# Routing MoE plus masked pooling on one core: where VectorE waits for the last operation of a table piece

## The chip, the cores and the metric

The kernel runs on one core of a Trainium2 chip. The metric is device time in microseconds (us); three runs of the kernel before gave 456.40, 456.65 and 457.12, so the median is 456.65. PE is TensorE, DVE is VectorE, ACT is ScalarE, POOL is GpSimd, SP is SyncE. "DVEq" in a row is DVE's own sequencer: register, load and wait instructions that it carries out itself and doesn't hand to the vector datapath.

## The reference, cut to what matters

The input is x, 8 batches of 512 tokens of 256 features. Layer 0: `u = zX * lap_x(x) + zY * lap_y(x) + zR * x * (1 - x)`, then a mixture of 8 experts with the best two chosen for each token:

```
logits = u @ router_weight; top_vals, top_idx = top_k(logits, 2); scores = softmax(top_vals)
gu = u @ gate_up_proj[e] + gate_up_proj_bias[e]            # 256 -> 512, gate and up interleaved
act = (clip(up, -7, 7) + 1) * min(gate, 7) * sigmoid(1.702 * min(gate, 7))
x = x + sum over the two experts of score * (act @ down_proj[e] + down_proj_bias[e])
```

Layer 1: scores `tanh(x @ W1 + b1) @ v`, a softmax over them under one of three masks (prefix, postfix, all but itself; one kind per batch), the pooled rows divided by the count of allowed positions, and an fp8-rounded product with `kernel`, whose result is added to x.

## The kernel before, in words

Stage A (0 to about 106 us) computes u, the router and each token's slots, and scatters the rows of u into per-expert regions of device memory. Stage B, the expert loop (about 106 to 317 us), takes NB = 71 blocks of 128 rows, two blocks to a step (`steps`; PAIRED is 68, the last three blocks stand alone). Stage C (from about 321 us) adds the weighted expert rows to X, computes the scores, the masked pooling and the fp8 product.

All engines run programs written out in full, one after the other, with semaphores between them. `instruction.then_inc(sem, 1)` raises a semaphore when the instruction is done; `dve.wait_ge(sem, n)` stands ahead of the next DVE instruction in program order, whatever that is.

What DVE does in iteration g of the expert loop (L1428 to L1444), in this order: `biased(g-1, 1)` (adds the bias to the second block of the last pair, L1337), `act_low(g-2)` (the low half of the transposed activation, L1360), `clipped(g-1)` (L1345, L1346), `rows_low(g+1)` (the low half of the transposed rows, L1325, and two small L1329), `activated(g-1)` (L1354), `biased(g, 0)` (L1337 for the first block), and then, for each block n of step g-1, `late_blocks(n)` and `tables_beside(n)`. These two do nothing for most n. For some even n they do one small piece of work that doesn't belong to the experts' own chain:

- `late_blocks`: n = 2, 4, 6, 8, 10, 12, 14: the experts and rows of the last 39 blocks, and the two weights of each token.
- `tables_beside`: n = 20 to 34 and 40 to 48 in twos: the kinds, scales, the rounded fp8 weights, the counts and the row and column tables of stage C.

Below, "piece n" is the work for block n. Pieces are short: one to four operations on DVE. Within a piece each operation that needs the one before it goes through `then` (semaphore `route_step`, L1211) or `table` (semaphore `table_step`, L1365). Both raise the semaphore by the instruction and write a wait for it behind the instruction at once. So in 17 of the pieces the last thing is a wait for the piece's own last operation.

Behind the piece DVE comes to `biased(g, 1)`, which begins with reading the number of the block's expert from on-chip memory into a register:

```
expert = dve.value_load(block_expert[0:1, n:n + 1], min_val=0, max_val=E - 1)   # L1335
dve.wait_ge(gu_psum, n + 1)                                                      # L1336
dve.tensor_tensor(gu_sum[...], gu_banks[...], gu_bias[:, ds(expert), :]..., ALU.add)   # L1337
```

[...]

PE's order in iteration g (L958 to L972): `gate_up(g, 0)`, `rows_transposed(g+1)`, `down(g-2)`, which needs `act_low(g-2)` of DVE (the wait shows at L949), `gate_up(g, 1)`, `act_transposed(g-1)`, which needs `activated(g-1)` of DVE (L940). ACT's order: `transposed_act(g-2)` (L680), `activate(g-1)` (L675), `rows_rounded(g+1)` (L670), `finish_down(g-2)` (L688). POOL scatters each finished block (L594), SP fetches the rows of blocks up to eight ahead (L486). When all blocks have been stored, SP loads `picks` (L524) and stage C begins.

PE waits for `table_step` once (L1002), up to the two steps of piece 20. Nobody but DVE waits for `route_step`.

Of the kernel before, what the change touches and what calls it, by code (L numbers as in the profile page):

```python
# [25 lines left out]
ALU = mybir.AluOpType  # L26
# [5 lines left out]
I32 = mybir.dt.int32  # L32
U32 = mybir.dt.uint32

P = 128
ALPHA, LIMIT = 1.702, 7.0
NEG = -1.0e30
EXPONENT_BITS = 0x7F800000
FP8_LEAST_NORMAL = 2.0 ** -6
FP8_GRID = 1.5 * 2.0 ** 20  # L40
# [39 lines left out]
def adaln_ffn_kernel(nc, x, zx, zy, zr, kinds, router_w, gate_up_w, gate_up_b, down_w, down_b,  # L80
                     w1, b1, v, ffn_k, in_scale, k_scale, ffn_b, out):
    B, S, H = x.shape
    E = router_w.shape[1]
# [23 lines left out]
    CAP = T + P  # L107
    CUT = B - 3
    FIRST_NB = (2 * CUT * S - E * (P - 1)) // P
    LATE_NB = NB - FIRST_NB  # L110
# [15 lines left out]
    with ExitStack() as ctx:  # L126
# [13 lines left out]
        tok_w = sb("tok_w", [P, 2, NT])  # L140
        ident = sb("ident", [P, P])

        with ExitStack() as ab:
# [13 lines left out]
            ends = sb("ends", [P, 10, E])  # L157
            ends_i = sb("ends_i", [P, 2, E], I32)
            base_f = sb("base_f", [P, E])
            odds = sb("odds", [P, 3, NT])  # L160
            blk_f = sb("blk_f", [P, NB])
# [39 lines left out]
            with ExitStack() as b_:  # L201
# [12 lines left out]
                kind_row = sb("kind_row", [1, 4, B])  # L214
# [3 lines left out]
                kind_col = sb("kind_col", [P, 8])  # L218
                spread = sb("spread", [P, QS, R], F32R)
                masks = sb("masks", [P, 3, P], BF16)  # L220
                zeros = sb("zeros", [P, P], BF16)
                counts = sb("counts", [P, 3, TB])
# [906 lines left out]
        def _(dve):  # L1129
# [78 lines left out]

            done = [0]

            def then(instruction):  # L1211
                done[0] += 1
                instruction.then_inc(route_step, 1)
                dve.wait_ge(route_step, done[0])

            def best_two(n):
# [68 lines left out]

            def late_blocks(n):
                late = blk_past[:, 0:LATE_NB]
                if n == 2:
                    dve.tensor_tensor(pads_at[:], ends[0:1, COUNT], base_f[0:1], ALU.add).then_inc(addresses_ready, 1)
                    rounded_down(P - 1, FULL)  # L1290
                if n == 4:
                    then(dve.tensor_tensor(ends_of(PADDED), ends_of(FULL), ends_of(TAKEN), ALU.subtract))
                    dve.memset(ends[:, JUMP, E - 1:E], float(E * CAP))
                    then(dve.tensor_tensor(ends[:, JUMP, 0:E - 1], ends[:, TAKEN, 1:E], ends[:, FULL, 0:E - 1],
                                           ALU.subtract))
                    then(dve.tensor_scalar(ends[:, JUMP, 0:E - 1], ends[:, JUMP, 0:E - 1], float(CAP), None, ALU.add))
                if n == 6:
                    then(dve.tensor_tensor_scan(ends_of(END), ends_of(ONE), ends_of(PADDED), 0.0, ALU.mult, ALU.add))
                    then(dve.tensor_tensor(late, blk_f[:, 0:LATE_NB].unsqueeze(2).broadcast_to([P, LATE_NB, E]),
                                           ends_of(END).unsqueeze(1).broadcast_to([P, LATE_NB, E]), ALU.is_ge))  # L1300
                if n == 8:
                    then(dve.tensor_reduce(blk_at[:, 0:LATE_NB], late, AX.X, ALU.add))
                    then(dve.tensor_scalar(block_is[:, FIRST_NB:NB], blk_at[:, 0:LATE_NB], float(E - 1), None, ALU.min))
                    dve.tensor_copy(block_expert[:, FIRST_NB:NB], block_is[0:1, FIRST_NB:NB]).then_inc(experts_ready, 1)
                if n == 10:
                    then(dve.tensor_tensor(late, late, ends_of(JUMP).unsqueeze(1).broadcast_to([P, LATE_NB, E]), ALU.mult))
                if n == 12:
                    then(dve.tensor_reduce(blk_at[:, 0:LATE_NB], late, AX.X, ALU.add))
                    then(dve.tensor_tensor(blk_at[:, 0:LATE_NB], blk_at[:, 0:LATE_NB], blk_f[:, 0:LATE_NB], ALU.add))
                    dve.tensor_scalar(block_row[:, FIRST_NB:NB], blk_at[0:1, 0:LATE_NB], ends[0:1, TAKEN, 0:1],  # L1310
                                      float(E * CAP), ALU.add, ALU.min).then_inc(addresses_ready, 1)
                if n == 14:
                    dve.wait_ge(odds_ready, 1)
                    then(dve.tensor_scalar(odds[:, 2], odds[:, 1], 1.0, None, ALU.add))
                    then(dve.reciprocal(tok_w[:, 0, :], odds[:, 2]))
                    then(dve.tensor_tensor(tok_w[:, 1, :], odds[:, 1], tok_w[:, 0, :], ALU.mult))

            x_low(0)
            straight(B, 2, step_a)
# [42 lines left out]

            tdone = [0]

            def table(instruction):  # L1365
                tdone[0] += 1
                instruction.then_inc(table_step, 1)
                dve.wait_ge(table_step, tdone[0])

            COLUMN, COLUMN_BATCH, ELSE, BELOW, ABOVE, OWN = range(6)  # L1370
            ROW, ROW_BATCH, KIND, PREFIX, POSTFIX, CLOZE, ONLY_POST, ONLY_PRE = range(8)

            def tables_beside(n):
                if n == 20:
                    dve.wait_ge(c_loaded, 16 * C_DMAS)
                    dve.memset(one[:], 1.0)
                    table(dve.tensor_copy(kind_row[:, 0, :], kind_row_i[:, 0, :]))
                    table(dve.tensor_copy(kind_rep[:], kind_row[:, 0, :].unsqueeze(1).unsqueeze(3).broadcast_to([1, QS, B, TB])))
                    assert tdone[0] == KIND_STEPS
                if n == 22:  # L1380
                    dve.tensor_scalar(kind_row[:, 1, :], kind_row[:, 0, :], 0.0, -2.0, ALU.is_equal, ALU.mult)
                    table(dve.tensor_scalar(kind_row[:, 2, :], kind_row[:, 0, :], 1.0, None, ALU.is_equal))
                    table(dve.tensor_tensor(kind_row[:, 1, :], kind_row[:, 1, :], kind_row[:, 2, :], ALU.subtract))
                if n == 24:
                    table(dve.tensor_scalar(kind_row_i[:, 1, :], kind_row[:, 1, :], 2.0, None, ALU.add))
                    table(dve.reciprocal(scales[:, 3:5], scales[:, 0:2]))
                    table(dve.tensor_tensor(scales[:, 2:3], scales[:, 0:1], scales[:, 1:2], ALU.mult))
                if n == 26:
                    table(dve.tensor_scalar(k_scaled[:], k_raw[:], scales[:, 4:5], None, ALU.mult))
                if n == 28:  # L1390
                    table(dve.tensor_scalar(k_grid[:].bitcast(I32), k_scaled[:].bitcast(I32), EXPONENT_BITS, None,
                                            ALU.bitwise_and))
                if n == 30:
                    table(dve.tensor_scalar(k_grid[:], k_grid[:], FP8_LEAST_NORMAL, FP8_GRID, ALU.max, ALU.mult))
                if n == 32:
                    table(dve.tensor_tensor(k_scaled[:], k_scaled[:], k_grid[:], ALU.add))
                if n == 34:
                    table(dve.tensor_tensor(k_quant[:], k_scaled[:], k_grid[:], ALU.subtract))
                if n == 40:
                    dve.wait_ge(tables, POOL_TABLES)  # L1400
                    table(dve.tensor_copy(counts[:, 0, :], counts_i[:]))
                    dve.tensor_scalar(counts[:, 1, :], counts[:, 0, :], -1.0, float(S + 1), ALU.mult, ALU.add)
                    table(dve.memset(counts[:, 2, :], float(S - 1)))
                if n == 42:
                    table(dve.reciprocal(counts[:], counts[:]))
                    table(dve.tensor_scalar(row_no[:, 0:1], row_no[:, 0:1], R - 1, None, ALU.bitwise_and))
                    table(dve.tensor_scalar(row_no[:, 1:2], row_no[:, 0:1], 2, None, ALU.logical_shift_right))
                if n == 44:
                    table(dve.tensor_scalar(col_no[:, 1, :], col_no[:, 0, :], 2, None, ALU.logical_shift_right))
                    dve.tensor_copy(kind_col[:, ROW:ROW_BATCH + 1], row_no[:])  # L1410
                    table(dve.tensor_copy(place[:, COLUMN:COLUMN_BATCH + 1], col_no[:]))
                if n == 46:
                    dve.tensor_scalar(place[:, ELSE], place[:, COLUMN_BATCH], kind_col[:, ROW_BATCH:ROW_BATCH + 1], NEG,
                                      ALU.not_equal, ALU.mult)
                    dve.tensor_scalar(place[:, BELOW], place[:, COLUMN], kind_col[:, ROW:ROW + 1], NEG, ALU.is_ge,
                                      ALU.mult)
                if n == 48:
                    dve.tensor_scalar(place[:, ABOVE], place[:, COLUMN], kind_col[:, ROW:ROW + 1], NEG, ALU.is_le,
                                      ALU.mult)
                    table(dve.tensor_scalar(spread[:, 0], place[:, COLUMN], kind_col[:, ROW:ROW + 1], None, ALU.is_equal))  # L1420

            rows_low(0)
            best_two(B - 1)
# [21 lines left out]


            dve.wait_ge(kind_psum, 1)
            table(dve.tensor_copy(kind_col[:, KIND:KIND + 1], kind_bank))
            kind = kind_col[:, KIND:KIND + 1]
            dve.tensor_scalar(kind_col[:, PREFIX:PREFIX + 1], kind, 0.0, NEG, ALU.not_equal, ALU.mult)  # L1450
# [194 lines left out]
```

## Time and profile before

| | |
|---|---|
| median of 3 runs | 456.65 us (456.40 to 457.12) |
| the profiled execution's own time | 458.76 us |
| its span | 457.0 us, 8319 instructions |
| PE busy | 365.7 us (80%), 2222 matmuls |
| DVE busy | 342.3 us (75%), 845 instructions |
| ACT busy | 211.3 us (46%) |
| POOL busy | 167.1 us (37%) |
| L1337, bias add | 71 times, 687 ns each, 16.9 us idle before them |

Busy shares are means over stages with different limits. Idle time in a row is that of the engine just before the instructions of the row; the name behind `<-` is what ended it, as inferred from the semaphores. A row of a timeline begins with the start and the duration in us; where two instructions of one line follow each other they can be merged ("x2").

### The profile page before, as it was taken

The page shows a single profiled execution, that of the slowest core. Times are in us where ns is not written, and L with a number is a line of the kernel's source. Part 1 is how long each engine was busy: PE and PEld are TensorE (multiplying, and loading weights), DVE is VectorE, ACT ScalarE, POOL GpSimd, SP SyncE. Part 2 cuts the span into 40 slices and gives each one's busy share as a digit, 9 for nine tenths or more (in the row PEclk, how much of TensorE's full clock was granted, in tenths as well). Part 3 has the DMA queues.
Part 4 walks back from the last instruction along what each step waited for, and adds up shares of the span by engine and source line. Part 5 has one row for each costly group of instructions (what it writes and reads, how often), then busy time and mean ns, then how long its engine had stood idle before and what let it go on. Part 6 is the DMA issues. An engine that isn't in the chain of part 4 may idle for free. (4 is left out here: it accounts for less than half of the span.)

```text
span 457.0 us, 8319 instructions
## 1 busy us (share of the span) xinstructions
PE 365.7 (80%) x2222; PEld 303.2 (66%) x2222; DVE 342.3 (75%) x845; ACT 211.3 (46%) x364; POOL 167.1 (37%) x186
## 2 busy tenths in 40 slices
PE   0969787668888899998999999995198849788871
PEld 0858666556777787777787888884145448677750
DVE  5688999967676777777777788875599654778872
ACT  3725444313333343343344444443165547799972
POOL 5026777777624333322233334344300023022121
PEclk9979898858999999999999999999579967899986
DMA  6986622256543333222232333110899100035445
GB/s 193 368 305 209 242 100 98 99 187 205 195 122 120 95 96 98 83 84 84 88 86 89 94 88 105 41 57 27 319 365 329 48 0 0 1 47 71 68 65 119
DMA packets 41326, 58.13 MB, mean 127 GB/s; under 512 B 6463, under 2 KB 30915, under 8 KB 41155
## 3 DMA queue, kind: packets, MB, share of 16 engines
q1 hardware_dynamic: 31106, 36.62, 25.5%
q0 software_dynamic: 10176, 20.98, 15.5%
q8 instruction: 21, 0.34, 0.3%
q14 instruction: 23, 0.18, 0.1%
HBM read 31.15 MB, written 27.34 MB: 128 GB/s over the span
## 5 line engine op out<-in xcount | busy, mean ns | idle before, releaser
L594 POOL DMA_INDIRECT y_rows<-outs,slot_dst x71 | 70.0, 986 | 126.7 <-ACT outs L688 113.9
L574 POOL DMA_INDIRECT regions<-flow,slots x64 | 68.7, 1074 | 43.2 <-DVE slots L1257 25.3
L910 PE MATMUL gu_banks<-gu_hi,rowT_hi 128*128 x142 | 60.3, 424 | 1.5 <-DVE rowT_lo L1325 1.5
L1337 DVE TENSOR_TENSOR gu_sum<-gu_banks,gu_bias 128x512 f32<-128x512 f32 x71 | 48.5, 687 | 16.9 <-PE gu_banks L910 3.9
L910 PE MATMUL gu_banks<-gu_hi,rowT_lo 128*128 x142 | 56.8, 400 | 0.0
L910 PE MATMUL gu_banks<-gu_lo,rowT_hi 128*128 x142 | 56.5, 398 | 0.0
L675 ACT ACTIVATE gelu<-gu_sum 128x512 f32<-128x512 f32 (+1 forms) x37 | 22.8, 615 | 59.5 <-DVE gu_sum L1345 59.5
L1325 DVE TENSOR_TENSOR rowT_lo<-bank,rowT_hi 128x512 fp32r<-128x512 f32 (+1 forms) x37 | 24.8, 669 | 30.8 <-ACT rowT_hi L670 30.8
L680 ACT ACTIVATE actT_hi<-bank 128x512 fp32r<-128x512 f32 (+1 forms) x37 | 21.5, 580 | 42.5 <-PE bank L940 42.5
L910 PE MATMUL bank<-dn_hi,actT_hi 128*128 x142 | 40.2, 283 | 0.0
L910 PE MATMUL bank<-dn_lo,actT_hi 128*128 x142 | 40.0, 281 | 0.0
L910 PE MATMUL bank<-dn_hi,actT_lo 128*128 x142 | 40.0, 281 | 0.0
L949 PE MATMUL bank<-dn_bias,ones 128*128 x71 | 23.3, 328 | 14.7 <-DVE actT_lo L1360 14.7
L688 ACT ACTIVATE outs<-bank 128x512 f32<-128x512 f32 (+1 forms) x37 | 21.5, 582 | 26.3 <-PE bank L910 26.3
L1467 DVE SCALAR_TENSOR_TENSOR X<-picks,tok_w,X 128x256 f32<-128x256 f32 x64 | 27.4, 480 | 6.1 <-DMA picks<-y_rows 5.6
L910 PEld LDWEIGHTS gu_banks<-gu_lo,rowT_hi 128*128 128x128 f32 x142 | 27.1, 191 | 6.6
L910 PEld LDWEIGHTS gu_banks<-gu_hi,rowT_hi 128*128 128x128 f32 x142 | 27.1, 191 | 5.8 <-issue 2.4
L614 POOL DMA_DIRECT2D out<-ffn_sum x7 | 10.3, 1470 | 56.3 <-DVE ffn_sum L1577 50.4
L910 PEld LDWEIGHTS gu_banks<-gu_hi,rowT_lo 128*128 128x128 f32 x142 | 27.2, 192 | 3.2
L1360 DVE TENSOR_TENSOR actT_lo<-bank,actT_hi 128x512 fp32r<-128x512 f32 (+1 forms) x37 | 24.6, 664 | 5.6 <-ACT actT_hi L680 5.6
L910 PEld LDWEIGHTS bank<-dn_hi,actT_lo 128*128 128x128 f32 x142 | 26.8, 189 | 0.0
L910 PEld LDWEIGHTS bank<-dn_hi,actT_hi 128*128 128x128 f32 x142 | 26.8, 188 | 0.0
(313 smaller groups left out, 959.3 us busy)
## 6 DMA issues: line engine op xcount, KB each, us to landing
rows<-regions SPq DMA_DIRECT2D x71, 136.0 KB, 2.2
picks<-y_rows SPq DMA_DIRECT2D x16, 512.0 KB, 8.4
X<-in_x SPq DMA_DIRECT2D x8, 512.0 KB, 8.9
gu_lo<-in_L_ffn_gate_up_proj SPq DMA_DIRECT2D x8, 512.0 KB, 7.9
out<-X SPq DMA_DIRECT2D x7, 512.0 KB, 6.6
out<-ffn_sum POOLq DMA_DIRECT2D x7, 512.0 KB, 5.6
dn_lo<-in_L_ffn_down_proj SPq DMA_DIRECT2D x8, 256.0 KB, 8.7
gu_bias<-_L_ffn_gate_up_proj_bias SPq DMA_DIRECT2D x1, 2048.0 KB, 9.1
```

The source lines that it names most:

```text
L574: pool.indirect_dma_start(out=regions, out_offset=bass.IndirectOffsetOnAxis(ap=slots[:, n, c, t:t + 1], axis=0), in_=flow[:, n % FS, t, :] ...
L594: pool.indirect_dma_start(out=y_rows, out_offset=bass.IndirectOffsetOnAxis(ap=slot_dst[:, m:m + 1], axis=0), in_=outs[:, m % UNROLL, :], i ...
L614: pool.dma_start(out_v[n], ffn_sum[:, n % 2], accum_op=ALU.add).then_inc(result_stored[n % 2], 16)
L675: a.activation(gelu[:, 0:cols], gate[:, 0:cols], ACT.Gelu_apprx_sigmoid).then_inc(gelu_ready, 1)
L680: a.activation(actT_hi[:, 0:cols], bank[5][:, 0:cols], ACT.Copy).then_inc(actT_hi_ready, 1)
L688: a.activation(outs[:, first:first + len(blocks), :].rearrange("p b h -> p (b h)"), bank[6 + g % 2][:, 0:len(blocks) * H], ACT.Copy).then_ ...
L910: mm = pe.matmul(acc, left[:, cols], right[:, ds(expert), part, :].rearrange("p e f -> p (e f)"), start=(not begun and part == 0 and left ...
L949: pe.matmul(acc, ones2[:], dn_bias[:, ds(expert), :].rearrange("r e h -> r (e h)"), start=True, stop=False)
L1325: dve.tensor_tensor(rowT_lo[:, g % 2, 0:cols], bank[4][:, 0:cols], rowT_hi[:, g % 2, 0:cols].bitcast(F32), ALU.subtract).then_inc(rowT_lo_ ...
L1337: dve.tensor_tensor(gu_sum[:, :, i * I:(i + 1) * I].unsqueeze(1), gu_banks[:, 2 * (g % 2) + i].rearrange("p (o i two) -> p o two i", o=1, ...
L1360: dve.tensor_tensor(actT_lo[:, 0:cols], bank[5][:, 0:cols], actT_hi[:, 0:cols].bitcast(F32), ALU.subtract).then_inc(actT_lo_ready, 1)
L1467: op = dve.scalar_tensor_tensor(out=X[:, n * TB + t, 0:H], in0=picks[:, s, t, c, :], scalar=tok_w[:, c, n * TB + t:n * TB + t + 1], in1=X[ ...
```

## The change

Two new helpers, `counted_route` and `counted`, raise the semaphore and count it, but write no wait. `then` and `table` now call them and add the wait. In 15 pieces (4, 6, 10, 14 of `late_blocks`; 22, 24, 26, 28, 30, 32, 34, 40, 42, 44, 48 of `tables_beside`) the last operation goes through the helper without a wait. A wait for everything counted so far is put at the beginning of `late_blocks` for n = 4 to 14 and of `tables_beside` for n = 22 to 48 (even n, those without a piece too), and one ahead of the first use behind the loop. Operations, their order, their operands and the count of semaphore steps are the same. Pieces 2, 8, 12, 20 and 46 keep their last operation as it was.

```diff
             done = [0]
 
-            def then(instruction):
+            def counted_route(instruction):
                 done[0] += 1
                 instruction.then_inc(route_step, 1)
+
+            def then(instruction):
+                counted_route(instruction)
                 dve.wait_ge(route_step, done[0])
...
             def late_blocks(n):
                 late = blk_past[:, 0:LATE_NB]
+                if n in range(4, 16, 2):
+                    dve.wait_ge(route_step, done[0])
...
-                    then(dve.tensor_scalar(ends[:, JUMP, 0:E - 1], ends[:, JUMP, 0:E - 1], float(CAP), None, ALU.add))
+                    counted_route(dve.tensor_scalar(ends[:, JUMP, 0:E - 1], ends[:, JUMP, 0:E - 1], float(CAP), None, ALU.add))
                 if n == 6:
                     then(dve.tensor_tensor_scan(ends_of(END), ends_of(ONE), ends_of(PADDED), 0.0, ALU.mult, ALU.add))
-                    then(dve.tensor_tensor(late, blk_f[:, 0:LATE_NB].unsqueeze(2).broadcast_to([P, LATE_NB, E]),
+                    counted_route(dve.tensor_tensor(late, blk_f[:, 0:LATE_NB].unsqueeze(2).broadcast_to([P, LATE_NB, E]),
                                            ends_of(END).unsqueeze(1).broadcast_to([P, LATE_NB, E]), ALU.is_ge))
...
-            def table(instruction):
+            def counted(instruction):
                 tdone[0] += 1
                 instruction.then_inc(table_step, 1)
+
+            def table(instruction):
+                counted(instruction)
                 dve.wait_ge(table_step, tdone[0])
...
             def tables_beside(n):
+                if n in range(22, 50, 2):
+                    dve.wait_ge(table_step, tdone[0])
...
                 if n == 28:
-                    table(dve.tensor_scalar(k_grid[:].bitcast(I32), k_scaled[:].bitcast(I32), EXPONENT_BITS, None,
+                    counted(dve.tensor_scalar(k_grid[:].bitcast(I32), k_scaled[:].bitcast(I32), EXPONENT_BITS, None,
                                             ALU.bitwise_and))
...
             dve.wait_ge(kind_psum, 1)
+            dve.wait_ge(table_step, tdone[0])
             table(dve.tensor_copy(kind_col[:, KIND:KIND + 1], kind_bank))
```

The other lines of the diff replace `then(` by `counted_route(` in pieces 10 and 14 and `table(` by `counted(` in the last operation of the eleven pieces named.

## Rows read from the trace of the kernel before

**Rows 1.** Busy time by window (start:end, length, PE, PEld, DVE, ACT, POOL, PEclk, DMA).
```profile
262.80:294.80 32.00, 32.00 (x206) 28.06 (x205) 25.85 (x55) 13.88 (x24) 11.81 (x12) 1.00 0.27 83
178.90:222.50 43.60, 39.37 (x240) 32.99 (x239) 31.77 (x76) 16.20 (x28) 13.78 (x14) 1.00 0.28 88
```

**Rows 2.** Waits from 115 to 320 us (total us, times, longest).
```profile
PE bank L949 <- DVE actT_lo L1360: 14.7, 21, 1.4
...
DVE gu_sum L1337 <- DVE spread L1420: 0.8, 1, 0.8
```

**Rows 3.** Timeline of DVE: steps without a piece (start, duration).
```profile
262.81 1.33 DVE L1337 TENSOR_TENSOR gu_sum<-gu_banks,gu_bias 128x512 f32<-128x512 f32 x2
...
268.11 1.37 DVE L1337 TENSOR_TENSOR gu_sum<-gu_banks,gu_bias 128x512 f32<-128x512 f32 x2
...
294.82 1.40 DVE L1337 TENSOR_TENSOR gu_sum<-gu_banks,gu_bias 128x512 f32<-128x512 f32 x2
```

**Rows 4.** Timeline of DVE: from piece 26 over piece 28.
```profile
191.21 0.68 DVE L1337 TENSOR_TENSOR gu_sum<-gu_banks,gu_bias 128x512 f32<-128x512 f32 x1
...
197.34 0.68 DVE L1337 TENSOR_TENSOR gu_sum<-gu_banks,gu_bias 128x512 f32<-128x512 f32 x1
197.94 0.42 DVE L1391 TENSOR_SCALAR k_grid<-k_scaled 128x512 int32<-128x512 int32 x1
199.13 0.69 DVE L1337 TENSOR_TENSOR gu_sum<-gu_banks,gu_bias 128x512 f32<-128x512 f32 x1 [0.78 <-DVE k_grid L1391]
```

**Rows 5.** Line 1335 in 198.3:199.0 (ns min/median/max, first and last start).
```profile
L1335 DVEq TENSOR_LOAD <-block_expert x1: 302/302/302, 198.4 to 198.4; - x1
```

**Rows 6.** Line 1335 in 196.0:196.7, ahead of the first block of that step.
```profile
L1335 DVEq TENSOR_LOAD <-block_expert x1: 305/305/305, 196.0 to 196.0; - x1
```

**Rows 7.** Timeline of DVE: piece 46.
```profile
252.09 0.23 DVE L1413 TENSOR_SCALAR place<-place,kind_col 128x32 f32<-128x32 f32 x1
252.24 0.23 DVE L1415 TENSOR_SCALAR place<-place,kind_col 128x32 f32<-128x32 f32 x1
252.38 0.68 DVE L1337 TENSOR_TENSOR gu_sum<-gu_banks,gu_bias 128x512 f32<-128x512 f32 x1
```

**Rows 8.** Timeline of DVE: piece 12.
```profile
150.49 0.20 DVE L1309 TENSOR_TENSOR blk_at<-blk_at,blk_f 128x39 f32<-128x39 f32 x1
150.72 0.24 DVE L1310 TENSOR_SCALAR block_row<-blk_at,ends 1x39 int32<-1x39 f32 x1
151.47 0.69 DVE L1337 TENSOR_TENSOR gu_sum<-gu_banks,gu_bias 128x512 f32<-128x512 f32 x1 [0.51 <-issue]
```

**Rows 9.** Line 1335 in 150.6:151.45, behind piece 12.
```profile
L1335 DVEq TENSOR_LOAD <-block_expert x1: 303/303/303, 150.7 to 150.7; - x1
```

**Rows 10.** Timeline of DVE: pieces 32 and 34.
```profile
209.47 0.68 DVE L1337 TENSOR_TENSOR gu_sum<-gu_banks,gu_bias 128x512 f32<-128x512 f32 x1
...
212.14 0.68 DVE L1360 TENSOR_TENSOR actT_lo<-bank,actT_hi 128x512 fp32r<-128x512 f32 x1
...
215.80 0.68 DVE L1337 TENSOR_TENSOR gu_sum<-gu_banks,gu_bias 128x512 f32<-128x512 f32 x1
216.40 0.69 DVE L1398 TENSOR_TENSOR k_quant<-k_scaled,k_grid 128x512 bf16<-128x512 f32 x1
218.22 0.69 DVE L1337 TENSOR_TENSOR gu_sum<-gu_banks,gu_bias 128x512 f32<-128x512 f32 x1 [1.13 <-PE gu_banks L910]
...
222.49 1.34 DVE L1337 TENSOR_TENSOR gu_sum<-gu_banks,gu_bias 128x512 f32<-128x512 f32 x2
```

**Rows 11.** Groups by line on DVE, 120 to 320 us: last operations of longer pieces.
```profile
L1299 DVE TENSOR_TENSOR blk_past<-blk_f,ends 128x312 f32<-128x312 f32 x1 | 0.5, 482 | 0.0
...
L1383 DVE TENSOR_TENSOR kind_row<-kind_row 1x8 f32<-1x8 f32 x1 | 0.2, 154 | 0.0
```

**Rows 12.** The chain that ended last, in order of time (start, us).
```profile
321.08 7.47 DMA picks<-y_rows
```

**Rows 13.** Busy time by window, in stage C (columns as in the first group).
```profile
324.00:329.00 5.00, 1.46 (x7) 1.49 (x8) 4.22 (x13) 1.39 (x2) 0.00 (x0) 0.50 0.97 363
```

More of the change, by code:

```diff
@@ L1305, in late_blocks @@
                 if n == 10:
-                    then(dve.tensor_tensor(late, late, ends_of(JUMP).unsqueeze(1).broadcast_to([P, LATE_NB, E]), ALU.mult))
+                    counted_route(dve.tensor_tensor(late, late, ends_of(JUMP).unsqueeze(1).broadcast_to([P, LATE_NB, E]), ALU.mult))
                 if n == 12:
@@ L1315, in late_blocks @@
                     then(dve.reciprocal(tok_w[:, 0, :], odds[:, 2]))
-                    then(dve.tensor_tensor(tok_w[:, 1, :], odds[:, 1], tok_w[:, 0, :], ALU.mult))
+                    counted_route(dve.tensor_tensor(tok_w[:, 1, :], odds[:, 1], tok_w[:, 0, :], ALU.mult))
             x_low(0)
@@ L1382, in tables_beside @@
                     table(dve.tensor_scalar(kind_row[:, 2, :], kind_row[:, 0, :], 1.0, None, ALU.is_equal))
-                    table(dve.tensor_tensor(kind_row[:, 1, :], kind_row[:, 1, :], kind_row[:, 2, :], ALU.subtract))
+                    counted(dve.tensor_tensor(kind_row[:, 1, :], kind_row[:, 1, :], kind_row[:, 2, :], ALU.subtract))
                 if n == 24:
@@ L1386, in tables_beside @@
                     table(dve.reciprocal(scales[:, 3:5], scales[:, 0:2]))
-                    table(dve.tensor_tensor(scales[:, 2:3], scales[:, 0:1], scales[:, 1:2], ALU.mult))
+                    counted(dve.tensor_tensor(scales[:, 2:3], scales[:, 0:1], scales[:, 1:2], ALU.mult))
                 if n == 26:
-                    table(dve.tensor_scalar(k_scaled[:], k_raw[:], scales[:, 4:5], None, ALU.mult))
+                    counted(dve.tensor_scalar(k_scaled[:], k_raw[:], scales[:, 4:5], None, ALU.mult))
                 if n == 28:
-                    table(dve.tensor_scalar(k_grid[:].bitcast(I32), k_scaled[:].bitcast(I32), EXPONENT_BITS, None,
+                    counted(dve.tensor_scalar(k_grid[:].bitcast(I32), k_scaled[:].bitcast(I32), EXPONENT_BITS, None,
                                             ALU.bitwise_and))
                 if n == 30:
-                    table(dve.tensor_scalar(k_grid[:], k_grid[:], FP8_LEAST_NORMAL, FP8_GRID, ALU.max, ALU.mult))
+                    counted(dve.tensor_scalar(k_grid[:], k_grid[:], FP8_LEAST_NORMAL, FP8_GRID, ALU.max, ALU.mult))
                 if n == 32:
-                    table(dve.tensor_tensor(k_scaled[:], k_scaled[:], k_grid[:], ALU.add))
+                    counted(dve.tensor_tensor(k_scaled[:], k_scaled[:], k_grid[:], ALU.add))
                 if n == 34:
-                    table(dve.tensor_tensor(k_quant[:], k_scaled[:], k_grid[:], ALU.subtract))
+                    counted(dve.tensor_tensor(k_quant[:], k_scaled[:], k_grid[:], ALU.subtract))
                 if n == 40:
@@ L1402, in tables_beside @@
                     dve.tensor_scalar(counts[:, 1, :], counts[:, 0, :], -1.0, float(S + 1), ALU.mult, ALU.add)
-                    table(dve.memset(counts[:, 2, :], float(S - 1)))
+                    counted(dve.memset(counts[:, 2, :], float(S - 1)))
                 if n == 42:
@@ L1406, in tables_beside @@
                     table(dve.tensor_scalar(row_no[:, 0:1], row_no[:, 0:1], R - 1, None, ALU.bitwise_and))
-                    table(dve.tensor_scalar(row_no[:, 1:2], row_no[:, 0:1], 2, None, ALU.logical_shift_right))
+                    counted(dve.tensor_scalar(row_no[:, 1:2], row_no[:, 0:1], 2, None, ALU.logical_shift_right))
                 if n == 44:
@@ L1410, in tables_beside @@
                     dve.tensor_copy(kind_col[:, ROW:ROW_BATCH + 1], row_no[:])
-                    table(dve.tensor_copy(place[:, COLUMN:COLUMN_BATCH + 1], col_no[:]))
+                    counted(dve.tensor_copy(place[:, COLUMN:COLUMN_BATCH + 1], col_no[:]))
                 if n == 46:
@@ L1419, in tables_beside @@
                                       ALU.mult)
-                    table(dve.tensor_scalar(spread[:, 0], place[:, COLUMN], kind_col[:, ROW:ROW + 1], None, ALU.is_equal))
+                    counted(dve.tensor_scalar(spread[:, 0], place[:, COLUMN], kind_col[:, ROW:ROW + 1], None, ALU.is_equal))
             rows_low(0)
```

## The prediction

> **What bounds the kernel now.** I read the busy time by window first, to find which engine sets the length of the expert loop. In the six steps without a piece from 262.8 us PE is busy 32.00 of 32.00 us; in the seven steps with pieces 22 to 34 it is busy 39.37 of 43.60 [rows 1]. [...] So the loop has two limits: PE where there is no piece, something else where there is one.
>
> The timeline of DVE gives the length of a step, measured from one `biased(g, 0)` (the first L1337 of a step) to the next. Without a piece: 262.81 to 294.82 for six steps, 5.33 each [rows 3]. With pieces 26, 28 and 30: 191.21 to 209.47, that is 18.26 for three, 6.09 each [rows 4, 10]. With 32 it is 6.33 and with 34 it is 6.69 [rows 10].
>
> The waits then say who is late. PE stood 14.7 us, in 21 places, before `down` until DVE's `act_low` was done [rows 2]; `act_low` follows `biased(g, 1)`, which follows the piece. And the bias add behind the piece stands 0.78 us after the piece's last operation: piece 28 ends at 197.94 + 0.42 = 198.36 and L1337 starts at 199.13 [rows 4]. The wait for piece 48's operation is the same 0.8 [rows 2]; there is such a row for 14 of the 15 changed pieces, and for the fifteenth, 34, the gap is 1.13 [rows 10].
>
> What fills the 0.78 us is not the vector datapath. The register load for the second block starts at 198.4 [rows 5], right when the wait for L1391 ends; the three register instructions behind it and the hand-over take the rest, about 0.74 from load to vector instruction. For the first block of the same step the load ran at 196.0 and its vector instruction started only at 197.34 [rows 4, 6]: there the sequencer was ahead by 1.34 - 0.74 = 0.60 us and its work cost nothing. The wait at the end of a piece takes this lead away.
>
> **The change, part by part.** (a) Fifteen waits go from in front of a register load. What happens then is seen in piece 46, which has no wait: operations at 252.09 and 252.24, L1337 at 252.38 [rows 7], no gap; each vector instruction even starts about 0.08 before the record of the one ahead ends (252.24 + 0.23 - 252.38 = 0.09). So the load runs beside the bias add of the first block. It can begin at about 196.8 in piece 28, is through at 197.5, and is needed at 198.3: a cover of 0.7 us, from `activated` and `biased(g, 0)` still running on the datapath. Were that cover gone, the 0.78 would come back.
>
> Seven pieces have no wait left at all (10, 26, 28, 30, 32, 34, 48). The new step on DVE is: first bias add to the piece's operation 0.60 (197.34 to 197.94), the operation less 0.08, second bias add to `act_low` 0.60, and from `act_low` to the next step 3.66 (212.14 to 215.80) [rows 4, 10]. With an operation of 0.42 that is 0.60 + 0.34 + 0.60 + 3.66 = 5.20, with one of 0.49 it is 5.26: both below PE's 5.33, so PE is late next, and the gain is cut there. For 26, 28 and 30 it is 18.26 - 3 x 5.33 = 2.27, 0.75 each, and I take the same 0.75 for 10 and 48: 3.75 together. Pieces 32 and 34 have operations of 0.68: 0.60 + 0.60 + 0.60 + 3.66 = 5.46. They take 209.47 to 222.49 = 13.02 now [rows 10] and 10.92 then: 2.10. The 0.36 that piece 34 has beyond 0.78 is in this: the row names PE as the releaser, but no other single-operation piece waits for PE there, so I take it for time of the sequencer, hidden like the rest; if it isn't, 1.74.
>
> (b) Eight pieces (4, 6, 14, 22, 24, 40, 42, 44) keep a wait between their operations. Piece 12 shows what remains: its last operation has a wait in front and none behind, it starts at 150.72, and the load starts at 150.7 as well [rows 8, 9], not earlier, though nothing behind the operation holds it. L1337 follows at 151.47, 0.78 after the operation that had been waited for. So here the load moves from the end of the last operation to its start, and the gain is the length of what stands behind the last inner wait: 0.48 in piece 6 (L1299), 0.15 in piece 22 (L1383) [rows 11], and 0.15 to 0.26 in the other six, of the same kind, 1.1 together; with 0.03 each for the wait's own delay, (0.48 + 0.15 + 1.1) + 8 x 0.03 = 1.95. These steps stay near 5.8 to 6.2, above PE's 5.33, so nothing cuts the gain.
>
> (c) 21 waits are added: 6 in `late_blocks`, 14 in `tables_beside`, one behind the loop. Each asks for an operation that ended a whole step earlier, more than 4 us before. Queued behind each is the piece's first operation and then the load and `biased(g, 1)`, for which PE's `down` waits two calls later. Their cost lies in the sequencer's lead of 0.60 [rows 4, 6], so I take nothing. From the two sides: a wait that is already met can't give time back, and if each took 0.03, as between the end of L1391 and the load, it would come to 21 x 0.03 = 0.6 with no cover at all.
>
> (d) The DMAs and the other queues. No DMA is moved, and no wait of SP, POOL or ACT. PE's only wait for `table_step` is for piece 20, which is unchanged. Whatever the loop gives is passed on: the loads of `picks` start when the last block is stored, and the chain that ended last runs through them, 321.08 and 7.47 long [rows 12]. They would start at about 313.3.
>
> **Sum.** 3.75 + 2.10 + 1.95 = 7.80 us. Against the profiled execution's own 458.76 that is 450.96. That execution lies 2.11 (0.5%) above the median of the runs, so for the median I take 456.65 - 7.8 = 448.85, rounded to 448.9.
>
> Low end of the gain: PE's idle time in the seven steps is only 43.60 - 39.37 = 4.23 [rows 1], while I take 0.2 + 0.2 + 2.25 + 2.1 = 4.7 out of them. If PE's busy records were all unavoidable, the gain would be a tenth smaller; with the 0.36 and the 0.6 of the added waits it is 7.0 - 1.0 = 6.0, time 450.7. High end with the same mechanism: each of the pieces 10 and 48 0.1 more and 0.1 more in each of the eight, 8.8, time 447.9.
>
> **The rivals.**
>
> (1) The wait was free, and something else takes its 0.78: no change, 456.65. For it: the idle rows name the last operation as releaser, which could be a plain write-to-read delay that the following wait for PE would only hide. Against it: within piece 12 a waiting operation follows its forerunner after 0.03 (150.49 + 0.20 to 150.72) [rows 8], so a wait by itself costs 0.03 and not 0.78, and piece 46 has no gap. [...] Chance 4%.
>
> (2) The sequencer runs ahead past waiting operations too, and all fifteen pieces lose the whole 0.78. Then the eight of (b) give about 0.54 more each, 4.3, which leaves them just above PE's 5.33: gain 12.1, time 444.5. For it: nothing in the program holds the load in piece 12. Against it: it started at 150.7 and not before, one case of one. [...] Chance 5%.
>
> (3) PE takes back half. The second block's products must be ready when DVE is early, and PE's order puts `down` ahead of them; if after a long piece PE starts each following step late, the small single-operation pieces give 0.3 and not 0.75, and 32 and 34 give 1.0: 1.5 + 1.0 + 1.95 = 4.5, time 452.2. Against it: steps without a piece reach 5.33 right behind piece 48 (262.81 to 268.11 is 5.30) [rows 3]. Chance 4%.
>
> (4) Slower: the clock. The denser loop, or the earlier start of stage C, leaves a stretch of PE's work at the lower level. It is there today after the loop, 0.50 in 324 to 329 where PE is busy only 1.46 of 5 us [rows 13] and DVE's chain hides it. [...] Against it: 32 us with PE busy throughout ran at 1.00 [rows 1]. Chance 2%.
>
> **How the numbers follow.** Forecast 448.9 with 85%, its own range 447.6 to 450.7; rivals 4%, 5%, 4% and 2% as above. I widen the low side of the gain for rival 3 and for what an execution of another instruction layout may add: range 447.3 to 451.7. It leaves out rivals 1, 2, 4 and part of 3 and of the forecast, a little under 2 in 10. Faster by over 0.2% (0.9 us, about what a measurement of this kernel can tell from no change): 94%; within 0.2%: 4%; slower: 2%.
>
> **What would show it.** In the profile after: L1337 behind pieces 10, 26 to 34 and 48 without idle time; behind 4, 6, 14, 22, 24, 40, 42 and 44 idle time of 0.3 to 0.65 with "issue" or the last operation as releaser, as in piece 12; the register load behind piece 28 starting before L1391. Steps 26, 28, 30 of 5.3, steps 32 and 34 of 5.45. PE's wait at L949 for DVE down from 14.7 by about 7. The loop's end, and `picks`, earlier by 7.8. I am wrong if the loads still start behind the last operation of the single-operation pieces, if steps 26 to 30 stay above 5.5, or if the loop ends 7.8 earlier and the end of the program does not.

## The result and the profile after

The changed kernel took 450.18 us, the median of 4 runs (450.03 to 451.54), and the kernel before 456.88 (456.40 to 457.44, 4 runs) beside it. The ratio is 0.9862, with a 95% interval from 0.9841 to 0.9883. The forecast was 448.9 in a range of 447.3 to 451.7, faster. The gain was put at 7.8 us and measured as 6.7 between the medians. The two profiled executions differ by 458.76 - 451.54 = 7.22.

The steps of the timeline say where it went. First DVE from piece 26 over piece 28 to piece 30 after, which answers to [rows 4] (start us, duration, engine, line, operation, and in brackets the idle time before). L1342 is the bias add that was L1337, L1401 is piece 28.

```profile
189.44 0.69 DVE L1342 TENSOR_TENSOR gu_sum<-gu_banks,gu_bias 128x512 f32<-128x512 f32 x1
...
194.74 0.69 DVE L1342 TENSOR_TENSOR gu_sum<-gu_banks,gu_bias 128x512 f32<-128x512 f32 x1
195.34 0.42 DVE L1401 TENSOR_SCALAR k_grid<-k_scaled 128x512 int32<-128x512 int32 x1
195.67 0.69 DVE L1342 TENSOR_TENSOR gu_sum<-gu_banks,gu_bias 128x512 f32<-128x512 f32 x1
...
200.10 0.69 DVE L1342 TENSOR_TENSOR gu_sum<-gu_banks,gu_bias 128x512 f32<-128x512 f32 x1
...
205.46 0.68 DVE L1342 TENSOR_TENSOR gu_sum<-gu_banks,gu_bias 128x512 f32<-128x512 f32 x1
...
210.93 0.68 DVE L1342 TENSOR_TENSOR gu_sum<-gu_banks,gu_bias 128x512 f32<-128x512 f32 x1
...
216.55 1.41 DVE L1342 TENSOR_TENSOR gu_sum<-gu_banks,gu_bias 128x512 f32<-128x512 f32 x2
```

The second bias add no longer stands 0.78 behind the piece's end: it starts at 195.67, 0.09 before L1401's record ends at 195.76. Steps 26, 28 and 30 are 5.30, 5.36 and 5.36 long (6.13, 6.07 and 6.07 before), step 32 is 5.47 (6.33), step 34 is 5.62 (6.69). The register load of that second block, line 1340, now runs ahead of the piece, where [rows 5] had it behind:

```profile
L1340 DVEq TENSOR_LOAD <-block_expert x1: 302/302/302, 194.2 to 194.2; - x1
```

It starts at 194.2, 1.1 us before L1401. The register instructions that stood between piece 28 and the bias add before, those of L1335 and then that of L1337, from 198.3 to 199.2:

```profile
L1335 DVEq TENSOR_LOAD <-block_expert x1: 302/302/302, 198.4 to 198.4; - x1
L1335 DVEq FUSED_REGOPS  x1: 190/190/190, 198.7 to 198.7; - x1
L1335 DVEq SEQ_ASSERT  x1: 23/23/23, 199.0 to 199.0; - x1
```
```profile
L1337 DVEq FUSED_REGOPS  x1: 57/57/57, 199.0 to 199.0; - x1
```

In a longer piece the wait between the operations stays, and the load moves only to where the last inner wait is met. Piece 40 shows it; its inner wait is for L1411, and the second fence has the load of line 1340 in that step:

```profile
227.85 0.17 DVE L1411 CAST counts<-counts_i 128x4 f32<-128x4 int32 x1
228.05 0.17 DVE L1412 TENSOR_SCALAR counts<-counts 128x4 f32<-128x4 f32 x1
228.16 0.06 DVE L1413 MEMSET counts<- 128x4 f32 x1
228.81 0.69 DVE L1342 TENSOR_TENSOR gu_sum<-gu_banks,gu_bias 128x512 f32<-128x512 f32 x1 [0.58 <-issue]
```

```profile
L1340 DVEq TENSOR_LOAD <-block_expert x1: 304/304/304, 228.1 to 228.1; - x1
```

The load starts with L1412, once L1411 is done (228.02), and L1342 follows 0.76 us after L1412's start. What L1412 and L1413 take of these 0.76 is hidden, and the rest is the idle time.

The waits in the loop after (us in all, times, longest), of the engines that count:

```profile
PE bank L949 <- DVE actT_lo L1365: 8.1, 13, 1.3
DVE gu_sum L1342 <- issue: 5.1, 10, 0.6
DVE gu_sum L1342 <- PE gu_banks L910: 2.7, 3, 1.3
DVE gu_sum L1342 <- DVE kind_rep L1388: 0.8, 1, 0.8
```

PE's wait for `act_low` fell from 14.7 us in 21 places [rows 2] to 8.1 in 13. The waits of 0.8 behind the changed pieces are gone (the one left is that of piece 20, which was not changed). Behind the eight longer pieces shorter ones, called "issue", are there instead; the other two of the ten, behind piece 12 and in the last steps, were there before.

The busy time of the whole loop, from the first bias add of the step with piece 2 to the one that follows the last full step. First before, then after (columns as in the first group of rows: window, length, PE, PEld, DVE, ACT, POOL, PEclk, DMA):

```profile
116.70:304.80 188.10, 175.20 (x1081) 149.38 (x1079) 142.75 (x334) 73.22 (x128) 67.66 (x76) 1.00 0.31 96
```
```profile
116.80:298.00 181.20, 174.61 (x1081) 149.73 (x1079) 143.44 (x335) 73.44 (x128) 69.98 (x76) 1.00 0.32 100
189.40:205.50 16.10, 16.10 (x104) 14.11 (x103) 13.55 (x32) 6.96 (x12) 6.40 (x6) 1.00 0.33 102
```

PE's idle time there went from 12.9 to 6.6 us. In the three steps from 189.4 PE is busy all the time, as it was only in steps without a piece [rows 1]. In exact stamps the loop took 188.17 us before and 181.17 after: 7.00 of the 7.22 us. It began 0.12 later after, and what follows it took 0.34 less. What the loop gave was passed on: the first load of `picks` is issued 320.13 - 313.33 = 6.80 us earlier, first before, then after:

```profile
320.13 4.40 SPq L524 DMA_DIRECT2D picks<-y_rows  x8
```
```profile
313.33 11.63 SPq L524 DMA_DIRECT2D picks<-y_rows  x12
```

The 321.08 of [rows 12] is not this start: the chain of before runs through the third of these loads, and two were issued ahead of it.

### The profile page after: what moved, and what is told of

Same layout as the page of the kernel before. It is cut to its first block and busy times, and to the rows that moved or that the text cites. A ratio compares the mean times of both kernels' runs of the same rounds, so it can differ in the third digit from the quotient of the medians.

```text
span 449.8 us, 8322 instructions
## 1 busy us (share of the span) xinstructions
PE 366.1 (81%) x2222; PEld 303.9 (68%) x2222; DVE 342.5 (76%) x845; ACT 211.7 (47%) x364; POOL 169.8 (38%) x186
## 5 line engine op out<-in xcount | busy, mean ns | idle before, releaser
L594 POOL DMA_INDIRECT y_rows<-outs,slot_dst x71 | 72.4, 1019 | 117.5 <-ACT outs L688 104.7
L1342 DVE TENSOR_TENSOR gu_sum<-gu_banks,gu_bias 128x512 f32<-128x512 f32 x71 | 48.7, 687 | 9.3 <-issue 5.3
L910 PE MATMUL bank<-dn_hi,actT_hi 128*128 x142 | 41.1, 289 | 0.0
```

The costliest lines, as they stand in the source:

```text
L594: pool.indirect_dma_start(out=y_rows, out_offset=bass.IndirectOffsetOnAxis(ap=slot_dst[:, m:m + 1], axis=0), in_=outs[:, m % UNROLL, :], i ...
L910: mm = pe.matmul(acc, left[:, cols], right[:, ds(expert), part, :].rearrange("p e f -> p (e f)"), start=(not begun and part == 0 and left ...
L1342: dve.tensor_tensor(gu_sum[:, :, i * I:(i + 1) * I].unsqueeze(1), gu_banks[:, 2 * (g % 2) + i].rearrange("p (o i two) -> p o two i", o=1, ...
```

## The experiments

My theory before them: the 0.78 us is the sequencer's register load, held back by a wait. The rivals still alive were that something else in a piece's end costs it, that the added waits cost something, and that PE or a neighbour takes back part. In what follows "the loop" is the stretch of 188.17 us before, by the profile of each run; the length of the whole comes from the medians. "Undo" means back to `then` or `table`, which carry the wait.

### The two parts and the added waits

`e1_single_pieces`: only the seven single-operation pieces changed.

```diff
-                    counted(dve.tensor_copy(place[:, COLUMN:COLUMN_BATCH + 1], col_no[:]))
+                    table(dve.tensor_copy(place[:, COLUMN:COLUMN_BATCH + 1], col_no[:]))
```
and the same in pieces 4, 6, 14, 22, 24, 40 and 42.

> Against the kernel before, only the seven pieces with no inner wait (10, 26, 28, 30, 32, 34, 48) lose their last wait; the added waits at the beginning of pieces stay. Theory A (the wait holds the sequencer's register load): 3.75 + 2.10 = 5.85 us by the prediction, 5.3 by the steps of the changed kernel's profile, so ratio 0.987 to 0.989. Theory B (the sequencer also passes operations that wait, the pieces with inner waits gave most): under 3 us. Theory C (a wait by itself costs its part, each of the fifteen the same): 7/15 of 6.7, 3.1 us.

`e2_longer_pieces`: the reverse, undone in pieces 10, 26, 28, 30, 32, 34 and 48, so that only the eight longer ones are changed.

```diff
-                    counted(dve.tensor_tensor(k_scaled[:], k_scaled[:], k_grid[:], ALU.add))
+                    table(dve.tensor_tensor(k_scaled[:], k_scaled[:], k_grid[:], ALU.add))
```

> Only the eight pieces with inner waits (4, 6, 14, 22, 24, 40, 42, 44) lose their last wait. Theory A: the load moves from the end to the start of the last operation, 1.9 us, ratio 0.996; behind piece 22 the second bias add stands idle for 0.6 us. Theory B: 0.78 us for each, 6 us, ratio 0.987, and no idle time. Theory C: 8/15 of 6.7, 3.6 us.

`e4_added_waits_only`: undone in all fifteen; the 21 added waits stay.

> The 21 added waits (at the beginning of pieces 4 to 14 and 22 to 48 and behind the loop) are there, and no wait is taken away. Theory A: they have long been met and lie in the sequencer's lead: 0 us, ratio 0.999 to 1.001. Rival (each costs 0.03 to 0.05 us of DVE's chain, which is where the missing 1.1 us of the gain went): 0.6 to 1.0 us slower, ratio 1.0015 to 1.0025.

Measured, beside a kernel before of 457.26 us (20 runs):

| | median us | ratio (95%) | loop us, against 188.17 |
|---|---|---|---|
| seven single pieces | 452.94 | 0.9916 (0.9896 to 0.9937) | 182.78, -5.40 |
| eight longer pieces | 455.64 | 0.9962 (0.9944 to 0.9979) | 186.24, -1.93 |
| added waits only | 457.22 | 1.0002 (0.9988 to 1.0016) | 187.98, -0.19 |

The added waits cost nothing that these runs can tell. The parts add up: 5.40 + 1.93 = 7.33 in the loop against 7.00 for the whole (7.33 when the whole was run again, e10 below), and 0.9916 x 0.9962 = 0.9878 against 0.9862, inside the interval. The longer pieces gave 1.93, forecast 1.95.

A length by the median follows the loop only to about 1 us: e1 lost 5.40 in the loop of its profiled execution and 4.3 between the medians, so its ratio of 0.9916 missed the 0.987 to 0.989 expected. The loop's length is on record for profiled executions alone, and e1's took 452.08 in all, 0.9 below its median; no run here says what the others spent the difference on. The loop is the finer measure and decides between the theories: 5.40 is theory A's 5.3.

### The load ahead of the wait

`e3_load_ahead`: all waits as in the kernel before, but the second block's register load is written ahead of the piece. This holds the price of the load apart from the price of the wait.

```diff
+            def expert_read(g, i):
+                n = steps[g][i]
+                return dve.value_load(block_expert[0:1, n:n + 1], min_val=0, max_val=E - 1)
...
-                expert = dve.value_load(block_expert[0:1, n:n + 1], min_val=0, max_val=E - 1)
+                expert = second.pop(g) if i else expert_read(g, 0)
...
+                    if len(steps[g]) == 2:
+                        second[g] = expert_read(g, 1)
```

> All waits stay as in the kernel before; only the register load of the second block's expert is written ahead of the piece, right behind the first bias add. Theory A: the wait then holds only the address instruction and the hand-over, some 0.2 to 0.25 us in place of 0.78; 0.5 us less in each of the fifteen pieces and in 12 and 20 too, cut where PE is the bound: 8 to 10 us less than before, ratio 0.978 to 0.983. Rival (the wait behind the operation costs by itself, whatever follows it): no change, the idle time behind the pieces stays 0.78.

Measured: 445.69 us, ratio 0.9743 (0.9729 to 0.9758); loop 176.04, that is 12.14 less. No wait is gone, and the gain is nearly twice that of the change. It is also more than the 8 to 10 expected, which counted the fifteen pieces, 12 and 20: these give 10.0, and the steps of pieces 2 and 8, which had been left out, 1.15 and 0.98 more. Piece 28 in this kernel (L1397; the bias add is L1343):

```profile
188.28 0.68 DVE L1343 TENSOR_TENSOR gu_sum<-gu_banks,gu_bias 128x512 f32<-128x512 f32 x1
188.88 0.42 DVE L1397 TENSOR_SCALAR k_grid<-k_scaled 128x512 int32<-128x512 int32 x1
189.44 0.69 DVE L1343 TENSOR_TENSOR gu_sum<-gu_banks,gu_bias 128x512 f32<-128x512 f32 x1
190.05 0.68 DVE L1366 TENSOR_TENSOR actT_lo<-bank,actT_hi 128x512 fp32r<-128x512 f32 x1
190.65 0.65 DVE L1351 TENSOR_SCALAR gu_sum<-gu_sum 128x512 f32<-128x512 f32 x1
```

Both loads of the step stand ahead of the piece now (the first and the last start of line 1335):

```profile
L1335 DVEq TENSOR_LOAD <-block_expert x2: 299/302/304, 187.0 to 187.7; - x2
```

One register instruction is left between the piece and the bias add, 57 ns long:

```profile
L1343 DVEq FUSED_REGOPS  x1: 57/57/57, 189.3 to 189.3; - x1
```

With the wait in place the bias add starts 0.14 us after the piece's end (189.30 to 189.44), not 0.78. Of the distance from first to second bias add, 1.79 before, e3 keeps 1.16 and the changed kernel 0.93. So of the 0.86 us the load behind the wait is 0.63 and the wait itself 0.23. e3 gains more in all because it reaches the whole of the longer pieces and the unchanged 2, 8, 12 and 20 as well. That the prediction put 12.1 on its second rival too is chance: its sum had other parts.

### How far the loop can go

`e5_change_and_load_ahead` is the changed kernel with the edit of e3. `e6_pieces_moved` keeps the waits of the kernel before and calls the pieces behind the clips instead of between the bias adds, so that neither a load nor PE's next operand stands behind them. `e7_moved_and_change` is e6's edit on the changed kernel:

```diff
+                    for n in steps[g - 1]:
+                        late_blocks(n)
+                        tables_beside(n)
...
-                if 0 <= g - 1 < STEPS:
-                    for n in steps[g - 1]:
-                        late_blocks(n)
-                        tables_beside(n)
```

> The change, and the register load of the second block's expert ahead of the piece. Theory A (a wait is dear only where a register load follows): nothing is held behind any piece but 20, whose last wait stays; the longer pieces lose their remaining 0.3 to 0.65 us of idle time, the steps with pieces come to 5.35 to 5.6, the loop from the first piece on is 174 to 175 us (188.2 before, 181.2 with the change, 176.0 with the load ahead alone): 13 to 14 us less than before, ratio 0.970. Rival (the load is not what the wait delays): no better than the change, 0.985.

> All waits as in the kernel before, the load in its old place; the calls of late_blocks and tables_beside stand behind the two clips instead of behind the first bias add, where DVE stands idle 0.85 us for ACT and where a vector instruction follows, not a register load. Theory A: a wait there costs 0.03 us, pieces up to 0.85 us are free and every step is PE's 5.35: loop about 172 us, 16 us less than before, ratio 0.965. Rival (a wait for one's own last operation costs 0.78 us wherever it stands): pieces of 0.4 us and more with their 0.78 overrun the idle time, steps of 5.7 to 6, ratio 0.975 to 0.985.

> The pieces moved as in the kernel with all waits, and the change on top. Theory A: the change is worth nothing there, because no register load stands behind the wait: same as the moved pieces alone within 0.2%, ratio 0.965. Rival (the wait costs by itself): 5 us less than the moved pieces alone.

Measured: ratios of 0.9698 (0.9653 to 0.9743), 0.9669 (0.9608 to 0.9729) and 0.9672 (0.9609 to 0.9736), loops of 173.13, 171.44 and 171.89 us. These three ran on another chip, where the kernel before took 480.83 us. Their loops start at 139 to 141 us and not at 115 to 117, so the extra time lies ahead of the loop, and only ratios and loops are read. e5 gave 15.0 in the loop, a little more than the 13 to 14 expected. With the pieces moved, the change of this case brings nothing more (0.9669 and 0.9672).

`e11_pieces_moved_again` is e6 once more and `e10_change_again` the changed kernel once more, on one chip with a kernel before of 457.42 us (11 runs).

> The changed kernel, once more, beside the moved pieces on one chip: ratio 0.986, as in the first measurement.

> The kernel with all its waits and the pieces behind the clips, once more, beside the changed kernel on one chip: loop 171.5 us, 9.7 us shorter than the change's 181.2; ratio 0.965, some 9 us below the changed kernel.

Measured: e10 450.42 us, 0.9861 (0.9830 to 0.9891), loop 180.85. e11 440.23 us, 0.9630 (0.9604 to 0.9657), loop 171.08: the fastest of all, 10 us under the changed kernel. Piece 30 in e11 (L1394) stands in time in which DVE waits for ACT anyway:

```profile
185.75 1.32 DVE L1337 TENSOR_TENSOR gu_sum<-gu_banks,gu_bias 128x512 f32<-128x512 f32 x2
187.34 0.69 DVE L1360 TENSOR_TENSOR actT_lo<-bank,actT_hi 128x512 fp32r<-128x512 f32 x1 [0.27 <-ACT actT_hi L680]
187.94 0.42 DVE L1345 TENSOR_SCALAR gu_sum<-gu_sum 128x512 f32<-128x512 f32 x1
188.28 0.55 DVE L1346 TENSOR_SCALAR up<-gu_sum 128x512 f32<-128x512 f32 x1
188.75 0.41 DVE L1394 TENSOR_SCALAR k_grid<-k_grid 128x512 f32<-128x512 f32 x1
189.62 0.69 DVE L1325 TENSOR_TENSOR rowT_lo<-bank,rowT_hi 128x512 fp32r<-128x512 f32 x1 [0.46 <-ACT rowT_hi L670]
```

And its busy time over the same loop:

```profile
115.80:286.90 171.10, 170.78 (x1081) 148.86 (x1079) 145.28 (x330) 73.34 (x128) 68.56 (x76) 1.00 0.34 106
```

PE is busy 170.78 of 171.10 us by its records. Nearly all steps are 5.3 to 5.4 long; that of piece 10 is still 5.80, with its clip L1345 stretched to 0.88 us, and that of piece 32 is 5.69, for which I have no cause. That no other order of work is faster is not shown. Of the 17.1 us between this loop and that of before the change gave 7.0.

### What stretches DVE's operations

The steps of e3 were longer than their parts said: in its piece 28 above, the clip L1351 took 0.65 us in place of 0.42. 22 of its clips took 0.48 us or more. 8 of them are of line 1351, and 7 of these 8 began 0.58 to 0.75 us after the start of a scatter on POOL. For piece 28 POOL's row is:

```profile
190.07 0.98 POOL L594 DMA_INDIRECT y_rows<-outs,slot_dst  x1 [0.30 <-issue]
```

`e8_scatter_later` is e3 with POOL held until DVE has done the two clips of the step two further on (`up_ready`), so that the second scatter of a step starts after the clips:

```diff
+                if m % 2 and m < PAIRED:
+                    pool.wait_ge(up_ready, min(step_of[m] + 3, STEPS))
```

> The kernel with the register load ahead of the pieces, and GpSimd issues the scatter of each pair's second block only when DVE has clipped the step two further on, so that no issue runs while a clip begins. Theory: in the kernel with the load ahead, a clip that begins 0.58 to 0.75 us after the start of a scatter's issue takes 0.49 to 0.65 us in place of 0.42 (8 of them at L1351 in the loop, and they lie on DVE's chain); with the scatter later these take 0.42 and the steps of pieces 24 to 34 lose 0.07 to 0.24 us each; loop 1.0 to 1.5 us shorter than 176.0, ratio 0.972. Rival (the clips' length has nothing to do with GpSimd): clips as before, loop 176.

Measured: 444.06 us, ratio 0.9730 (0.9702 to 0.9757), loop 175.07, 0.97 less than e3. The two clips over the loop (ns min/median/max), first in e3, then in e8, where lines 1351 and 1352 are 1353 and 1354:

```profile
L1351 DVE TENSOR_SCALAR gu_sum<-gu_sum x35: 282/418/658, 117.7 to 298.9; 128x512 f32<-128x512 f32 x32, 128x256 f32<-128x256 f32 x3
L1352 DVE TENSOR_SCALAR up<-gu_sum x35: 288/423/556, 118.0 to 299.1; 128x512 f32<-128x512 f32 x32, 128x256 f32<-128x256 f32 x3
```
```profile
L1353 DVE TENSOR_SCALAR gu_sum<-gu_sum x35: 282/416/419, 117.9 to 298.2; 128x512 f32<-128x512 f32 x32, 128x256 f32<-128x256 f32 x3
L1354 DVE TENSOR_SCALAR up<-gu_sum x35: 286/419/422, 118.2 to 298.4; 128x512 f32<-128x512 f32 x32, 128x256 f32<-128x256 f32 x3
```

The maxima of 658 and 556 ns fall to 419 and 422: the stretching belongs to what POOL does beside it. For the time of the whole the two intervals overlap, so what it is worth is told by the loop alone, 1 us, the low end of what was expected.

`e9_pool_tables_later` is the changed kernel with POOL's own table operations eight blocks later.

```diff
-                if m == 10:
+                if m == 18:
```

> The changed kernel with GpSimd's own table work (two memsets, three iotas, four selects) moved from its block 10 to its block 18. Theory: the 0.28 us by which the step of piece 10 stayed above 5.33 (its two small scalar_tensor_tensor took 0.35 and 0.33 in place of 0.21 while GpSimd did its selects) go away, that step takes 5.35, and a later one, four steps on, gets them. Rival (the step of piece 10 is long for another reason): it stays at 5.6.

Measured once: 450.01 us, loop 180.91. Step 10, 5.61 after and 5.80 in e10, became 5.28; steps 18 and 20, 5.43 and 6.14 after, became 5.85 and 6.23. The excess moved with POOL's tables. In e10 the clip of piece 10's step, and what POOL did beside it:

```profile
143.91 0.88 DVE L1350 TENSOR_SCALAR gu_sum<-gu_sum 128x512 f32<-128x512 f32 x1
```
```profile
143.56 0.98 POOL L594 DMA_INDIRECT y_rows<-outs,slot_dst  x1 [0.30 <-issue]
144.52 0.41 POOL L580 MEMSET zeros<- 128x128 bf16 x1
```

and in e9 the same clip in the same step, then in the step to which POOL's tables had moved:

```profile
143.12 0.42 DVE L1350 TENSOR_SCALAR gu_sum<-gu_sum 128x512 f32<-128x512 f32 x1
...
166.32 0.88 DVE L1350 TENSOR_SCALAR gu_sum<-gu_sum 128x512 f32<-128x512 f32 x1
```

## Why the prediction was right, and where it was short

The mechanism held, and the sum was 0.8 us too large. By the prediction's steps, in the profiled executions (us saved):

| step | forecast | measured | in e10 |
|---|---|---|---|
| (a) pieces 10, 26, 28, 30, 48 | 3.75 | 0.53 + 0.83 + 0.71 + 0.71 + 0.68 = 3.46 | 3.29 |
| (a) pieces 32 and 34 | 2.10 | 0.86 + 1.07 = 1.93 | 1.82 |
| (b) eight longer pieces | 1.95 | 0.26 + 0.48 + 0.23 + 0.16 + 0.11 + 0.18 + 0.16 + 0.27 = 1.85 | 1.98 |
| (c), (d) and the unchanged steps | 0 | -0.24 | +0.24 |
| loop | 7.80 | 7.00 | 7.33 |

**(a), the mis-sized term.** 0.46 of the 0.8 us is here, and 0.74 in e10. Piece 10 gave 0.53 and not 0.75, because its shorter step lies beside POOL's tables; e9 shows it, with a step of 5.28 once they are moved away. Pieces 28, 30 and 48 came out at 5.36 each and not 5.33: the prediction took PE's bound from six steps of which the first two follow a step that PE had not filled, 5.31 each; the later ones are 5.34 to 5.36. Piece 34 is 0.16 longer than its sum of 5.46. In e10 it is 5.73, and there the clip of 0.68 at 212.6 accounts for it; in the changed kernel itself the clip took 0.42, and `act_low` started 0.74 instead of 0.60 after the bias add, at 212.87. That is 0.03 after ACT's `actT_hi` was done, and ACT had waited for PE:

```profile
211.57 0.63 PE L940 MATMUL bank<-ident,up 128*128 128x128 f32 x4
212.24 0.60 ACT L680 ACTIVATE actT_hi<-bank 128x512 fp32r<-128x512 f32 x1 [1.44 <-PE bank L940]
```

PE's transposes began 0.64 us after the step's first bias add here and 0.32 in e10. Why they were later here is open.

**The 0.36 of piece 34.** The prediction took the extra idle time for the sequencer's, against the row, which names PE. The trace of before bears that out: between the load's last register instruction (start 217.7) and that of the bias add (218.1) stand 0.40 us, where piece 30's two stand at 205.0 and 205.1.

```profile
L1335 DVEq SEQ_ASSERT  x1: 23/23/23, 217.7 to 217.7; - x1
...
L1337 DVEq FUSED_REGOPS  x1: 57/57/57, 218.1 to 218.1; - x1
```

PE was not late. The last product of that block ended at 215.90 + 0.40 = 216.30:

```profile
215.90 0.40 PE L910 MATMUL gu_banks<-gu_lo,rowT_hi 128*128 x1
```

e3 says the same: with the load ahead the idle time behind piece 34 is 0.14, as behind the others, and the 1.25 behind piece 2 and the 0.94 behind piece 8, which the profile of before also puts down to PE, are 0.14 and none.

After, a pause of the same 0.39 us stands in that step (register instructions at 210.7 and 211.3) and costs nothing, since the vector datapath has work: L1342 starts at 212.13 without idle time.

**(b)** was right in size and kind: the idle time behind the eight is 0.49 to 0.60, and 0.27 behind piece 6 with its longer last operation, named "issue", as in piece 12 [rows 8]. So was **(c)**, by e4. **(d)**: the kind was right, since what the loop gave reached the loads of `picks` (6.80) and the end (7.22). The start of 313.3 was hit by luck, by two errors that cancel: the prediction took 321.08 for the loads' start, which was 320.13, and its 7.8 was 1.0 more than the 6.80 that came. From 320.13 it would have said 312.3.

**The unchanged steps** took 0.24 us more in the one execution and 0.24 less in the other, so they hold no effect that these runs tell from scatter. What moves them is seen in piece 8, whose step was 0.26 shorter after: one of its operations, L1303, took 0.45 us before and 0.18 after, and the step is as long as before again in e10.

**The rivals.** No change (1) is refuted by e3 and e4: the same wait costs 0.78 us ahead of a register load and 0.14 without it. Running ahead past waiting operations (2) is refuted by piece 40 above and by e2, which gave 1.93 and not the some 6.3 that (b) would have given (1.95 + 4.3). A return to PE (3) would have cost 3.3; what it cost is the step of 5.36 in place of 5.33, seen above. The clock (4) stayed at 1.00 over the loop in every kernel, e11 with PE busy 170.78 of 171.10 us among them; over what follows the loop its mean was 0.85 before and 0.83 after, and that stretch took 0.34 us less. Between vector instructions a wait costs little: behind one the next instruction starts 0.03 us after the end in piece 12, without one 0.09 before it in piece 46, so the wait costs 0.12 there. Where the next thing is a register load, the wait behind piece 28 cost its step 0.86 us.

## What to carry to other kernels

Look at what stands behind a wait on the engine's queue, not only at what it waits for: with a register load behind the wait the next vector instruction started 0.78 us after the piece's end (piece 28 before), with the load ahead of it 0.14 us (e3). Writing the load ahead of the wait gave more (12.1 us in the loop) than moving the wait (7.0), and placing the extra work where the engine waits for another anyway gave the most (17.1) and made the wait's place indifferent. When a step is bound by another engine once the stall is gone, take that engine's rate from steps that have long been bound by it (5.34 to 5.36 us here), not from the first ones behind a stall (5.31).

## What the runs showed of the hardware

- A DVE clip of 128x512 takes 0.42 us and was stretched to 0.49 to 0.68 when it began 0.56 to 0.75 us after POOL had started on a scatter, and to 0.88 where POOL's table operations followed the scatter; with the second scatters held back none of 70 was stretched (maximum 422 ns). It cost nothing in the steps of blocks 56 to 63: 5.35 to 5.36 us in e3, where the second clip took 0.54 to 0.55, and 5.35 in e8, where both took 0.42. The step of piece 28 went from 5.67 in e3 to 5.44 in e8.
- DVE's sequencer pauses by 0.39 to 0.40 us in the steps of pieces 8 and 34, before and after, with no wait that was still open. The profile puts it down to PE. There are more such pauses: in the records of before 447 and 703 instructions of DVE stand ahead of these two, and pauses of 0.43 to 0.44 between a semaphore instruction and the register load behind it stand at 573, 829 and 957, ahead of a first bias add, where they cost nothing. In e11 such pauses stand at 830 and 956. So they come some 128 instructions apart, or a multiple of that, whatever the instruction does, which speaks for the place in the list and not for the operation. The cause is not shown; no experiment was made for it.
- PE's busy time for the same 1081 matmuls, at a granted clock of 1.00, fell from 175.2 us before to 174.6 after and 170.8 in e11 (the ends of its records are modelled). So the busy time that this loop had with its stalls was no floor for it: the steps of pieces 22 to 34 gave 4.44 us where PE had been idle for 4.23 [rows 1], which the prediction's low end took for a possible bound.
